# In an LSTM-like recurrence, one product moves from VectorE to GpSimd, and the cell tanh moves from PSUM to SBUF

## The reference

```python
def step(carry, xs):
    h, c = carry
    xi_t, xf_t, xg_t, xo_t = xs
    i_t = jax.nn.sigmoid(xi_t + h @ V_i)
    f_t = jax.nn.sigmoid(xf_t + h @ V_f)
    g_t = jnp.tanh(xg_t + h @ V_c)
    o_t = jax.nn.sigmoid(xo_t + h @ V_o)
    c_new = h * c + i_t * g_t
    h_new = o_t * jnp.tanh(c_new)
    return ((h_new, c_new), h_new)
```

## Time and profile before

| what | value |
|---|---|
| median of 3 runs | 465.47 us (465.15 to 467.15) |
| span of the profiled execution | 462.5 us |
| PE, DVE, ACT, POOL busy | 314.4, 270.5, 209.8, 20.3 us |
| granted TensorE clock, mean | 0.624 |

### The profile page before, as it was taken

How to read it: one execution, slowest core, us unless ns; L and a number is a source line. 1 busy time by engine, 2 the same in 40 slices (tenths; PEclk the granted TensorE clock), 3 DMA queues, 4 the chain that set the end, 5 groups by cost and what they waited for, 6 DMA issues and landing times.

```text
span 462.5 us, 12630 instructions
## 1 busy us (share of the span) xinstructions
PE 314.4 (68%) x4036; PEld 247.6 (54%) x4041; DVE 270.5 (58%) x1794; ACT 209.8 (45%) x1169; POOL 20.3 (4%) x39
## 2 busy tenths in 40 slices
PE   4799889898766666666666655666666666656664
PEld 2466448534655555555555555555555555555553
DVE  3965445554455665566555655566556655665564
ACT  1587254263544444444444444444444444444442
POOL 8900000000000000000000000000000000000000
PEclk9899998999755555555555555555555555555555
DMA  8300000000000000000000000000000000000000
GB/s 316 161 3 1 0 1 1 0 1 0 3 1 0 0 0 0 0 0 0 0 0 0 0 0 0 0 0 0 0 0 0 0 0 0 0 0 0 0 0 11
DMA packets 2827, 5.77 MB, mean 12 GB/s; under 512 B 1408, under 2 KB 1792, under 8 KB 2816
## 3 DMA queue, kind: packets, MB, share of 16 engines
q1 hardware_dynamic: 2384, 4.55, 2.6%
q10 hardware_dynamic: 432, 1.08, 0.6%
HBM read 5.50 MB, written 0.13 MB: 12 GB/s over the span
## 4 chain that ended last, share of the span: by engine, by line
PE 42%; ACT 35%; DVE 13%; issue 7%; POOL 1%; DMA 1%; SPq 0%; DVEq 0%; POOLq 0%
PE bank L653 25%; ACT bank L374 15%; DVE ha L921 10%; ACT bank L367 9%; ACT go L371 5%; ACT gi L365 3%; PE bank L412 2%; PE bank L421 2%; PE bank L432 2%; PE bank L384 1%; POOL bias L228 1%; PE bank L584 1%; DMA bnd<-in_bands 1%; PE bank L596 1%; PE bank L545 1%
## 5 line engine op out<-in xcount | busy, mean ns | idle before, releaser
L653 PE MATMUL bank<-ha,vparts 128*128 128x1 f16 x2304 | 102.6, 168 | 126.5 <-DVE ha L921 126.5
L653 PEld LDWEIGHTS bank<-ha,vparts 128*128 128x128 bf16 x2304 | 81.8, 106 | 149.4 <-DVE ha L921 149.4
L365 ACT ACTIVATE gi<-bank 128x1 f32<-128x1 f32 x256 | 43.9, 172 | 187.1 <-PE bank L653 187.1
L918 DVE TENSOR_SCALAR gos<-go 128x1 f32<-128x1 f32 x256 | 39.4, 154 | 97.6 <-ACT go L371 97.6
L374 ACT ACTIVATE bank<-bank,hc,gi 128x1 f32<-128x1 f32 x256 | 82.9, 324 | 0.0
L653 PE MATMUL bank<-hb,vlead 128*128 128x1 f16 x768 | 59.2, 169 | 0.0
L921 DVE SCALAR_TENSOR_TENSOR ha<-bank,go 128x1 f16<-128x1 f32 x256 | 41.1, 161 | 29.7
L648 PE MATMUL bank<-x,w5s 128*128 (+1 forms) x198 | 56.4, 360 | 0.2 <-DVE x L762 0.2
L461 PE MATMUL bank<-ones,w5s 128*128 128x8 f32 x198 | 55.8, 356 | 0.0
L925 DVE SCALAR_TENSOR_TENSOR hb<-bank,gos,ha 128x1 f16<-128x1 f32 x256 | 55.5, 217 | 0.0
L923 DVE SCALAR_TENSOR_TENSOR cell<-bank,gi,hc 128x1 f32<-128x1 f32 x256 | 53.2, 208 | 0.0
(11 more groups left out here) (212 smaller groups left out, 278.1 us busy)
## 6 DMA issues: line engine op xcount, KB each, us to landing
w3s<-in_w SPq DMA_DIRECT2D x1, 804.0 KB, 10.2
ltr<-in_later SPq DMA_DIRECT2D x1, 709.0 KB, 7.5
bias<-in_positions ACTq DMA_DIRECT2D x1, 704.0 KB, 5.1
bias<-in_positions SPq DMA_DIRECT2D x1, 704.0 KB, 6.2
w2s<-in_w SPq DMA_DIRECT2D x1, 640.0 KB, 8.8
w5s<-in_w SPq DMA_DIRECT2D x1, 576.0 KB, 11.2
w0s<-in_w ACTq DMA_DIRECT2D x1, 336.0 KB, 3.7
w1s<-in_w SPq DMA_DIRECT2D x1, 256.0 KB, 7.7
```

Source lines behind the costliest of these rows:

```text
L365: act.activation(gi[:], bank[pre + 1][:, at:at + 1], ACT.Sigmoid)
L653: m = mm(bank[3 * parity + k][:, at:at + 1], weight, h, start=False, stop=False, skip_group_check=True)
L918: ts(gos[:], o, HSCALE, None, ALU.mult)
```

## The change

The cell tanh `tc` becomes a column of SBUF instead of PSUM. `gos` gets two columns, used in turn, and raises a semaphore `o_scaled`. GpSimd gets a loop of its own: in each step it waits for `o_scaled` and for `tanh_c`, multiplies `tc` with `gos` in float32 into `h32`, and raises `h32_ready`. VectorE's `hb` is then a tensor_tensor, `h32` minus `ha`, behind an added wait for `h32_ready`. The order on VectorE stays.

```diff
-        gi, go, gos = sb("gi", [P, 1]), sb("go", [P, 2]), sb("gos", [P, 1])
+        gi, go, gos = sb("gi", [P, 1]), sb("go", [P, 2]), sb("gos", [P, 2])
...
-        gt, tc = bank[6][:, 0:1], bank[7][:, 0:1]
+        gt, tc, h32 = bank[6][:, 0:1], sb("tc", [P, 1])[:], sb("h32", [P, 2])
...
+            with pool.Fori(0, N, STEPS_IN_BODY) as base:
+                for u in range(STEPS_IN_BODY):
+                    t, two = base + u, slice(u % 2, u % 2 + 1)
+                    pool.wait_ge(on("o_scaled"), t + 1)
+                    pool.wait_ge(on("tanh_c"), t + 1)
+                    pool.tensor_tensor(h32[:, two], tc, gos[:, two], ALU.mult).then_inc(on("h32_ready"), 1)
...
-                    ts(gos[:], o, HSCALE, None, ALU.mult)
+                    ts(gos[:, u % 2:u % 2 + 1], o, HSCALE, None, ALU.mult).then_inc(on("o_scaled"), 1)
...
                     dve.wait_ge(on("ha_ready"), t + 2)
-                    stt(out=hb[:], in0=tc, scalar=gos[:], in1=ha[:], op0=ALU.mult, op1=ALU.subtract)\
-                        .then_inc(on("hb_ready"), 1)
+                    dve.wait_ge(on("h32_ready"), t + 1)
+                    tt(hb[:], h32[:, u % 2:u % 2 + 1], ha[:], ALU.subtract).then_inc(on("hb_ready"), 1)
```

## The result

The changed kernel takes 511.97 us (median; 510.78 to 513.44), the kernel before 465.78 in the same comparison: a ratio of 1.098, 95% interval 1.095 to 1.101. It is 46 us slower, 0.18 us for each of 256 steps. Slower was forecast, with 486 us; the size was missed by more than half. The profiled execution itself took 513.44 us, with a span of 511.6.

The account below looks back on a forecast made before the run. The prediction took the recurrence to be bound by latency, 1.32 us a step; hb's way over GpSimd adds 0.08 us, 20.5 us over 256 steps, so 462.5 + 20.5 + 3.0 gives 486 us; range 466 to 518.

Parts of the forecast that it names:

- the two paths that meet at the load of hb: Before hb's first weight load: tanh, ha, hb against tanh, ha, nine loads; the hb path is later by only 0.02 us.
- hb's way over GpSimd as the late one: Tanh, GpSimd product, hb: hb starts 0.14 us later, less 0.06 for its shorter instruction, +0.08 us a step.
- The cap on any gain: A shorter hb gives at most 0.02 us a step, 5 us, since ha's nine loads bind next on TensorE.
- idle time ahead of the hb loads: A sign in the profile after: TensorE idles between the ha and hb loads, near 0.10 us.
- The blocking rival: VectorE's ha, with two SBUF inputs, and GpSimd's product hold each other: +0.20 us a step, 517 us; chance 0.16.
- the sum's own upper bound: All small prices of tanh, wake, product and return at their high ends: +0.17 us a step, 509 us.
- the one on the waits: On GpSimd ahead of the product: the wait for gos, done 0.09 us ahead of the tanh, costs nothing.
- VectorE's added wait: Ahead of hb, from GpSimd's product to VectorE: a handover of 0.03 to 0.04 us, taken as 0.03.
- The product: GpSimd's one-column multiply takes 0.26 us, from the line through wider tensor_tensors; bounds 0.19 to 0.30.
- The tanh in SBUF: Writing the cell tanh to SBUF instead of PSUM costs 6 ns, with 0 and 37 as bounds.
- POOL's wake behind one wait: From the tanh's end to the start of GpSimd's product: 0.07 us, bounds 0.03 to 0.08.
- then nothing changes: A sign of being wrong: if GpSimd's product row is near 190 ns, the kernel's time stays as before.

Follow-up runs that it names:

- experiment 1: The kernel before with only the cell tanh's destination changed, from PSUM to SBUF; GpSimd has no part in the recurrence: 472.26 us, ratio 1.014.
- experiment 2: The changed kernel, but VectorE computes hb itself from tc, gos and ha, and waits for GpSimd's product only ahead of hc: 472.46 us, 1.015.
- experiment 9: The changed kernel, but an extra GpSimd operation takes the first wait (o_gate); the product of tc and o waits for the tanh alone: 493.85 us, 1.059.
- experiment 8: The kernel before with hb = tc - ha as a tensor_tensor, factor gos left out, so the low part of h is wrong: 462.64 us, 0.992.
- experiment 10: The changed kernel with VectorE's wait for ha_ready moved ahead of cell, so hb has only the wait for GpSimd's product: 491.94 us, 1.056.
- experiment 11: The changed kernel with both the separate GpSimd operation for the first wait and the ha_ready wait moved ahead of cell: 490.73 us, 1.055.
- experiment 5: The changed kernel with the o gate written to PSUM instead of SBUF, so ha and hs have one SBUF input each: 511.54 us, 1.098.
- experiment 13: The kernel before with the wait for ha_ready written twice ahead of hb: 483.63 us, 1.037.
- experiment 14: The kernel before with a wait for gos (o_scaled) added between gos and the tanh wait, ahead of ha: 485.70 us, 1.043.
- experiment 7: The changed kernel with GpSimd's product replaced by a memset of h32 to zero, waits compared with constants; low part of h wrong: 480.46 us, 1.032.
- experiment 6: The changed kernel without gos: GpSimd waits for o_gate, multiplies tc with o, and VectorE makes hb as h32 * 256 - ha: 511.30 us, 1.097.

## Why the prediction missed

**Right, by its steps.** The sign and the mechanism: the two paths that meet at the load of hb, and hb's way over GpSimd as the late one (experiments 1, 2 and 9). The cap on any gain: "at most 0.02 us a step, 5 us"; experiment 8 gave 3.7 us. (That hb starts at 301.03 "since it reads ha" is not the only reading: it also starts 0.12 behind cell's start at 300.91, and in experiments 10 and 11 cell alone let it start 0.13 to 0.14 behind. The sum is the same either way.) ha's read from SBUF at no cost (163 ns against 161), and hb as a tensor_tensor at 159 (164). ha not on the path any more, and idle time ahead of the hb loads. That its size fits, "near 0.10" against 21.9 us / 256 = 0.086, is luck: counted as the forecast counted it, from where a tenth load could start (301.55 + 0.24 = 301.79), it is 0.16. The blocking rival fell, although its 517 us lies near the measured time, nearer than the forecast: its two signs, POOL starting only at ha's end or ha's row growing, are both absent (POOL starts 0.05 before ha's end, ha has 163 ns), and experiments 2 and 5 exclude it. So it is also luck that 512 us lies inside the stated range: the sum's own upper bound is 509, and the range went to 518 only for this rival. The Trainium skill's rule (SBUF — State Buffer, section on the two separate sides), that a VectorE operation with two SBUF inputs and a GpSimd operation that reads SBUF lock each other out, would have held hb in experiment 2 until GpSimd's product ended and so made it slower than experiment 1; hb starts 0.04 after ha's end in both, and they differ by 0.2 us. For operations of one column no run here shows that lock.

**The step that failed** is the one on the waits. The prediction said of POOL: "So POOL's first wait is over before its second, and costs nothing", with a reserve only for a first wait that is handled more than 0.09 us late. The first wait is over in time (gos ends at 301.18, the tanh at 301.30), but with two waits the wait for the tanh is no longer carried by the product, and the product starts 0.14 after the tanh where 0.07 was put in. The prediction also took VectorE's added wait as one more handover of 0.03 to 0.04; hb carries the wait for `ha_ready`, the late wait for the product stands on an instruction ahead, and it is 0.10. Each costs 0.07 us a step, 0.14 together: by the sum 36 us of the 46. Experiments 9 and 10 took them away one at a time and gave 18 and 20 us back; experiments 13 and 14 made the same cost in the kernel before, 18 and 20 us. That both gone would give 36 was expected in experiment 11 (476 us) and is not shown, since cell then held hb.

**Terms that were mis-sized.** The product: 0.26 forecast, 0.190 measured. The line through the tensor_tensors of 176 and 384 columns was the wrong guide; the line through the casts gave 0.19. That is 18 us too much, and it hid half of the failed step. The tanh in SBUF: 6 ns forecast, 27 measured, inside the bounds 6 to 37, 5 us too little. hb: 5 ns, 1 us. POOL's wake behind one wait: 0.07 forecast, 0.07 measured (experiment 9), so that this term was right by itself. Together: 0.08 forecast + 0.14 (waits) - 0.07 (product) + 0.02 (tanh) + 0.01 (hb) = 0.18.

Two of the prediction's own signs of being wrong appeared. The tanh's row changed by more than 10 ns. And POOL's row is 190 ns, to which it had tied "then nothing changes"; the time changed by 46 us all the same, since that sentence too left the waits out.

The sum's upper bound, 509 us, was built from prices of the parts and no case for the waits, although one sentence named the place. No version over GpSimd beat the kernel before. The best that uses its product is experiment 11, 490.7 us, where cell holds hb. Without that, a way over GpSimd would still have 0.07 for the wake, 0.19 for the product, 0.03 for the return and 6.9 us for the tanh's destination (an estimate from the rows: the 476 us expected in experiment 11), and what a shorter hb can win is under 4 us.

**Open.** Where the late wait has to stand is shown; why an instruction of its own costs 0.07 us is not. Neither is a kernel in which only the order of GpSimd's two waits is changed. The memset started 0.03 us earlier than the product behind the same waits; why wasn't tried.

## What to carry to other kernels

On a path bound by latency, price an operation that moves to another engine as two handovers plus its row, and count how many waits stand directly ahead of each instruction. One of them is carried by the operation and is cheap; if the one that is met last is another, it cost 0.07 of a step of 1.32 us here, however early the rest were met. So ask the trace for the lines of the waits, and see that the late wait has no row of its own. Where two are needed, let an operation that is not on the path carry the early one, as in experiment 9, and check what that operation then holds up (experiment 11). Before moving anything, look for the path that is nearly as long as the one being shortened; here it left 4 us to win.

## What the runs showed that was not expected

- An operation whose last-met wait stands on an instruction of its own ahead of it starts 0.07 us later than one that carries that wait, on VectorE (0.03 to 0.10 and 0.11, 0.04 to 0.11 after the releaser's end) and on GpSimd (0.07 to 0.14). An early wait in that place cost nothing (466.0 against 465.9 us).
- The sigmoid of o is such a case on ScalarE, in the changed kernel and before: its wait for `hc_ready` is a row of its own (L377), and in the changed kernel it starts 0.10 after the end of hc (302.20 to 302.30). So the 0.10 us that the prediction counted as left over there was used up.
- A one-column float32 tensor_tensor on GpSimd takes 190 ns, about 30 more than VectorE's (159), and a memset 99 (experiment 7).
- The cell tanh, with scale and bias from SBUF, takes 324 ns into PSUM and 352 into SBUF. The sigmoid of o takes 199 ns into SBUF in the changed kernel and in experiment 6, and 165 into PSUM in the steady stretch of experiment 5:

```profile
L379 ACT ACTIVATE bank<-bank 128x1 f32<-128x1 f32 x201 | 33.1, 165 | 0.0
```

- VectorE and GpSimd on one-column operands of SBUF did not slow each other: 472.3 us without and 472.5 with 256 products on GpSimd.
